# Packing two tile words for TensorE, and four block numbers for VectorE, into one register load in the relation passes of a graph network kernel

## The reference

```python
def rgcn_layer(x, src, dst, etype, W, W_root, b, num_rels):
    h = jnp.einsum('ni,rio->rno', x, W)
    msg = h[etype, src]
    seg = dst * num_rels + etype
    sums = jax.ops.segment_sum(msg, seg, num_segments=N * num_rels)
    cnt = jax.ops.segment_sum(jnp.ones(msg.shape[0], x.dtype), seg, num_segments=N * num_rels)
    mean = sums / jnp.maximum(cnt, 1.0)[:, None]
    agg = mean.reshape(N, num_rels, do).sum(axis=1)
    return agg + x @ W_root + b
# _L3_gnn_ref:
h = rgcn_layer(x, src, dst, edge_type, W1, root1, b1, NUM_RELS)
h = jax.nn.relu(h)
return rgcn_layer(h, src, dst, edge_type, W2, root2, b2, NUM_RELS)
```

## Time and profile before

| | us |
|---|---|
| Median of 3 runs | 3515.31 (3507.41 to 3517.1) |
| The profiled execution | 3496.86 |
| Its span, first to last instruction | 3494.7 |
| PE busy | 2004.6 (57%) |
| DVE busy | 1933.7 (55%) |
| POOL busy | 1461.6 (42%) |

### The profile page before, as it was taken

The page is one execution under the profiler, slowest core; times in us unless marked ns, Lnnn a source line. Parts: engine busy times, 40 slices in busy tenths (PEclk is TensorE's granted clock), DMA queues, the critical chain, the costliest instruction groups (busy, mean ns, idle before and its releaser), DMA issues.

```text
span 3494.7 us, 58674 instructions
## 1 busy us (share of the span) xinstructions
PE 2004.6 (57%) x12959; PEld 1187.5 (34%) x12959; DVE 1933.7 (55%) x6993; ACT 431.4 (12%) x904; POOL 1461.6 (42%) x1520
## 2 busy tenths in 40 slices
PE   3777799898145777777763499333333333333336
PEld 1333354444123555554531278111111111111116
DVE  5999868961345667666764466333333333333334
ACT  1555411111100000000000045000000000000000
POOL 2000000000565665556665411566656666665660
PEclk8988899999557899999985599555555555555557
DMA  2455400421112222222221111111111111111110
GB/s 69 114 114 132 109 1 1 155 81 43 48 42 54 66 68 68 66 66 68 68 57 40 36 56 74 58 43 43 43 42 44 43 43 43 43 43 41 44 43 26
DMA packets 187665, 204.28 MB, mean 58 GB/s; under 512 B 110588, under 2 KB 155277, under 8 KB 187234
## 3 DMA queue, kind: packets, MB, share of 16 engines
q0 software_dynamic: 46560, 95.32, 11.0%
q1 hardware_dynamic: 120918, 85.48, 8.9%
q10 hardware_dynamic: 19884, 19.74, 2.3%
HBM read 141.49 MB, written 39.29 MB: 52 GB/s over the span
## 4 chain that ended last, share of the span: by engine, by line
PE 41%; issue 29%; DVE 20%; another core or an unknown queue 3%; ACT 2%; SPq 1%; DVEq 1%; DMA 1%; POOL 1%; ACTq 1%; POOLq 0%
PE banks L685 16%; PE banks L660 9%; DVE hi_hot L1316 6%; DVE adj L1637 4%; PE banks L590 4%; PE banks L575 4%; PE banks L729 2%; DVE lo_hot L1324 2%; PE banks L741 2%; PE banks L776 1%; DVE zT L1620 1%; DVE hot L1611 1%; DVEq L1635 1%; DVE deg_in L1484 1%
## 5 line engine op out<-in xcount | busy, mean ns | idle before, releaser
L846 POOL DMA_INDIRECT adj<-table,adj x1453 | 1388.4, 956 | 945.8 <-SPq L462 583.0
L685 PE MATMUL banks<-adj,hot 128*128 x3908 | 776.2, 267 | 1118.4 <-issue 772.3
L1637 DVE TENSOR_TENSOR adj<-adj,banks 128x129 f32 x1954 | 564.3, 289 | 1222.1 <-PE banks L685 848.8
L685 PEld LDWEIGHTS banks<-adj,hot 128*128 128x128 f16 x3908 | 402.1, 103 | 1497.8 <-issue 1405.1
L660 PE MATMUL banks<-split,zT 128*128 128x256 f16 x2775 | 435.3, 293 | 161.9 <-DVE zT L1620 87.1
L1611 DVE TENSOR_SCALAR hot<-adj 128x128 f16<-128x128 f16 x1954 | 513.1, 263 | 1.4
L660 PEld LDWEIGHTS banks<-split,zT 128*128 128x128 f16 x2775 | 256.0, 104 | 221.3 <-issue 65.4
L547 PE MATMUL banks<-hi_hot,lo_hot 128*128 128x400 f16 x977 | 248.2, 383 | 100.7 <-DVE hi_hot L1316 64.4
L1620 DVE TENSOR_TENSOR zT<-zT,blocks 128x640 f16<-128x640 f16 x555 | 269.3, 485 | 0.0
L1316 DVE TENSOR_SCALAR hi_hot<-iota,zT 128x400 f16<-128x400 f16 x977 | 254.5, 331 | 21.0 <-PE banks L547 20.9
L590 PE MATMUL banks<-adj,split 128*128 128x512 f16 (+1 forms) x1078 | 216.8, 359 | 0.0
(11 more groups left out here) (252 smaller groups left out, 1549.4 us busy)
## 6 DMA issues: line engine op xcount, KB each, us to landing
adj<-table,adj POOLq DMA_INDIRECT x1453
adj_copy<-adj SPq DMA_DIRECT2D x24, 800.0 KB, 3.9
zT<-scr_sources ACTq DMA_DIRECT2D x111, 160.0 KB
adj<-adj_copy SPq DMA_DIRECT2D x6, 2176.0 KB, 15.9
table<-adj SPq DMA_DIRECT2D x25, 512.0 KB, 2.6
adj<-adj_copy SPq DMA_DIRECT2D x1, 3072.0 KB, 10.4
adj<-adj_copy SPq DMA_DIRECT2D x3, 1024.0 KB, 15.4
table<-split SPq DMA_DIRECT2D x6, 256.0 KB, 2.3
```

The source lines that it names most:

```text
L685: m = e.matmul(bank[j % NSUM][:, 0:b - a], hot[:, j % NHOT, :], edge[:, a:b], start=(q == 0), stop=(q == 1), skip_group_check=True)
L846: e.indirect_dma_start(gath[:, (t + which) % NG, 0:2 * D], None, table, bass.IndirectOffsetOnAxis(ap=index[:, which, t:t + 1].bitcast(U32) ...
L1637: e.tensor_tensor(a, a, bank[j % NSUM][:, 0:D + 1], ALU.add).then_inc(accumulated, 1)
```

## The change

The plan now packs the words before they go to DRAM. Two 16-bit tile words make one 32-bit word (`pairs_i`, 489 of them), and four block numbers of 8 bits make one (`quads_i`, 245). This is done by eight DVE instructions on one partition after the last `expand`, and two small memsets before it; SP's writes of the two lists wait for them (`pairs_set`). In the passes PE loads 8 registers every 16 steps, DVE 8 registers every 32 steps. Each step then cuts its field out: PE shifts (on odd steps) and masks with 0xFFFF, then masks the tile number; the maximum with 1 is gone. DVE shifts (on three steps of four) and masks. SP's `relay` and POOL's gathers are as before.

```diff
+    JP, JQ = -(-JA // 2), -(-JA // 4)
...
             e.wait_ge(rows_set, len(PICKS))
             e.dma_start(scr_c, out_c[:, :]).then_inc(plan_out, 16)
-            e.dma_start(scr_w, rows_i[:, 0, :]).then_inc(plan_out, 16)
-            e.dma_start(scr_t, rows_i[:, 1, :]).then_inc(plan_out, 16)
+            e.wait_ge(pairs_set, 2)
+            e.dma_start(scr_w, quads_i).then_inc(plan_out, 16)
+            e.dma_start(scr_t, pairs_i).then_inc(plan_out, 16)
...
             def scatter(which):
                 base = which * JA
                 for j in range(JA):
-                    if j % WORDS == 0:
-                        n = min(WORDS, JA - j)
-                        e.load(tile_regs[0:n], tile_row[:, j:j + n])
+                    w = j // 2
+                    if j % (2 * WORDS) == 0:
+                        n = min(WORDS, JP - w)
+                        e.load(tile_regs[0:n], tile_row[:, w:w + n])
                     if which == 0:
                         select_part(j)
-                    e.reg_alu(least, tile_regs[j % WORDS], (1 << BUF_LOG2) - 1, ALU.bitwise_and)
-                    e.reg_alu(least, least, 1, ALU.max)
+                    word = tile_regs[w % WORDS]
+                    if j % 2:
+                        e.reg_alu(field, word, 16, ALU.logical_shift_right)
+                        word = field
+                    e.reg_alu(field, word, 0xFFFF, ALU.bitwise_and)
+                    e.reg_alu(least, field, (1 << BUF_LOG2) - 1, ALU.bitwise_and)
                     e.wait_ge(hot_set, base + j + 1)
                     e.wait_ge(landed[which], least)
                     if which:
                         c = e.snap(least, min_val=1, max_val=T) % NG
                     else:
-                        word = e.snap(tile_regs[j % WORDS], min_val=1, max_val=((NG + NGX) << BUF_LOG2) - 1)
+                        word = e.snap(field, min_val=1, max_val=((NG + NGX) << BUF_LOG2) - 1)
                         c = word // (1 << BUF_LOG2)
...
             expand(len(PICKS) - 1)
+            fields = rows_i[:, 1, 0:2 * JP].rearrange("a (j h) -> a j h", h=2)
+            e.wait_ge(sums_read, len(PICKS))
+            e.wait_ge(own_dve, own.n)
+            e.tensor_scalar(high_i, fields[:, :, 1], 16, None, ALU.logical_shift_left).then_inc(own_dve, 1)
+            e.wait_ge(own_dve, own.up())
+            e.tensor_tensor(pairs_i, fields[:, :, 0], high_i, ALU.bitwise_or).then_inc(pairs_set, 1)
+            windows4 = rows_i[:, 0, :].rearrange("a (j h) -> a j h", h=4)
+            for h in range(1, 4):
+                e.tensor_scalar(parts_i[:, h, :], windows4[:, :, h], 8 * h, None, ALU.logical_shift_left).then_inc(own_dve, 1)
+                own.up()
+            e.wait_ge(own_dve, own.n)
+            e.tensor_tensor(parts_i[:, 0, :], windows4[:, :, 0], parts_i[:, 1, :], ALU.bitwise_or).then_inc(own_dve, 1)
+            e.wait_ge(own_dve, own.up())
+            e.tensor_tensor(parts_i[:, 1, :], parts_i[:, 2, :], parts_i[:, 3, :], ALU.bitwise_or).then_inc(own_dve, 1)
+            e.wait_ge(own_dve, own.up())
+            e.tensor_tensor(quads_i, parts_i[:, 0, :], parts_i[:, 1, :], ALU.bitwise_or).then_inc(pairs_set, 1)
...
-            regs = [e.alloc_register(f"window{i}") for i in range(REGS)]
+            regs = [e.alloc_register(f"window{i}") for i in range(WORDS)]
+            field = e.alloc_register("window_field")
...
                 for j in range(JA):
-                    if j % REGS == 0:
-                        n = min(REGS, JA - j)
-                        e.load(regs[0:n], win[0:1, j:j + n])
+                    w = j // 4
+                    if j % (4 * WORDS) == 0:
+                        n = min(WORDS, JQ - w)
+                        e.load(regs[0:n], win[0:1, w:w + n])
                     e.wait_ge(scattered, base + j + 1)
                     if j:
                         e.wait_ge(accumulated, base + j)
-                    c = e.snap(regs[j % REGS], min_val=0, max_val=NW - 1)
+                    word = regs[w % WORDS]
+                    if j % 4:
+                        e.reg_alu(field, word, 8 * (j % 4), ALU.logical_shift_right)
+                        word = field
+                    e.reg_alu(field, word, 0xFF, ALU.bitwise_and)
+                    c = e.snap(field, min_val=0, max_val=NW - 1)
```

More of the change, by code:

```diff
@@ L111, in gnn_stack @@
         adj_copy = nc.dram_tensor("adj_copy", [NB, P, NP], F16, kind="Internal").ap()
-        scr_w = nc.dram_tensor("scr_windows", [1, JA], I32, kind="Internal").ap()
-        scr_t = nc.dram_tensor("scr_tiles", [1, JA], I32, kind="Internal").ap()
+        scr_w = nc.dram_tensor("scr_windows", [1, JQ], I32, kind="Internal").ap()
+        scr_t = nc.dram_tensor("scr_tiles", [1, JP], I32, kind="Internal").ap()
         scr_l = nc.dram_tensor("scr_last", [T], I32, kind="Internal").ap()
@@ L178, in gnn_stack @@
         out_c = carve([P, JA])
-        rows_i = carve([1, 2, JA], I32)
+        rows_i = carve([1, 2, 4 * JQ], I32)
+        quads_i = carve([1, JQ], I32)
+        parts_i = carve([1, 4, JQ], I32)
+        pairs_i = carve([1, JP], I32)
+        high_i = carve([1, JP], I32)
         last_f = carve([P, TB])
@@ L232, in gnn_stack @@
         spare = rows[:, :, :].rearrange("p k d -> p (k d)")
-        win, tile_row, last_row = (spare[32 * i:32 * i + 1, 0:n].bitcast(I32) for i, n in enumerate((JA, JA, T)))
+        win, tile_row, last_row = (spare[32 * i:32 * i + 1, 0:n].bitcast(I32) for i, n in enumerate((JQ, JP, T)))
         assert JA <= 9 * D and T <= 9 * D
@@ L308, in gnn_stack @@
         selected, part_summed, copied = (sem(n) for n in ("selected", "part_summed", "copied"))
-        squared, square_sum, bound_set, bound_root, scale_set, w_high, w_low = (
-            sem(n) for n in ("squared", "square_sum", "bound_set", "bound_root", "scale_set", "w_high", "w_low"))
+        pairs_set, squared, square_sum, bound_set, bound_root, scale_set, w_high, w_low = (
+            sem(n) for n in ("pairs_set", "squared", "square_sum", "bound_set", "bound_root", "scale_set", "w_high", "w_low"))
         row_scaled, row_turned, row_high, row_low, x_turned, x_high, x_low = (
@@ L649, in _ @@
             least = e.alloc_register("least_landed")
+            field = e.alloc_register("field")
             def select_part(j):
@@ L1289, in _ @@
                         expand(c - 1)
-            expand(len(PICKS) - 1)
+            if JA % 4:
+                e.memset(rows_i[:, 0, JA:4 * JQ], 0).then_inc(own_dve, 1)
+                own.up()
+            if JA % 2:
+                e.memset(rows_i[:, 1, JA:2 * JP], 1).then_inc(own_dve, 1)
+                own.up()
+            expand(len(PICKS) - 1)
+            fields = rows_i[:, 1, 0:2 * JP].rearrange("a (j h) -> a j h", h=2)
[7 more added lines that the diff above has]
+                e.tensor_scalar(parts_i[:, h, :], windows4[:, :, h], 8 * h, None, ALU.logical_shift_left).then_inc(own_dve, 1)
+                own.up()
+            e.wait_ge(own_dve, own.n)
[4 more added lines that the diff above has]
+            e.tensor_tensor(quads_i, parts_i[:, 0, :], parts_i[:, 1, :], ALU.bitwise_or).then_inc(pairs_set, 1)
             pad = win_pad[:, :, :].rearrange("p a b -> p (a b)")
```

## The result

The changed kernel takes 3580.69 us (median of 4 runs, 3568.52 to 3588.41) against 3516.2 for the kernel before on the same chip (4 runs, 3507.41 to 3522.09): ratio 1.0179, 95% interval 1.0154 to 1.0204. That is 64 us slower, well beyond the 0.3% that a measurement can tell. The profiled execution is the fastest, 3568.52 us, with a span of 3566.4: 71.7 more than before.

The account below looks back on a forecast made before the run. Gathers were taken to set the pace of both passes by slowing PE's sequencer. Steps +10, DVE's loads -5 and plan +3 gave +8 us on 3515, so 3523 us, "no difference", range 3450 to 3590.

Parts of the forecast that it names:

- the two slower rivals: In the passes: every sequencer instruction costs (3583 us), or DVE's addition comes too late (3559 us); chance 0.18 each.
- Plan, +3 (2 to 4): End of the plan: eight DVE packing instructions on one partition add 2.8 us, taken as +3, between 2 and 4.
- PE's shift 0.088 us, a load every sixteenth step: PE in both passes: 976 shifts cost +86 us, 122 fewer loads at 0.64 us give -78, together +8.
- DVE's loads 0.59 us: DVE in the passes: 62 loads shrink from 2.10 to 0.59 us, -94 us of sequencer time, of which -5 counted.
- The waiting for one-hots: Sign in the second pass: PE's waits for DVE's one-hots fall below 70.8 us, with no gain from it.
- the term of the steps, +10: Both passes: PE's extra step work, +3 us scaled by time or +18 by instruction count, taken as +10; DVE's instructions left out.
- the late-addition rival: In the passes: DVE's masks and shifts between PE's product and the addition delay it, +41 us, 3559; chance 0.18.
- The sign that the prediction named for it: In the passes: if DVE's addition comes too late, PE's waits for additions grow by tens of microseconds.
- Loads count in full: Rival in the passes: fewer, smaller loads on PE and DVE save time, -83 us in full, -40 likelier, 3475; chance 0.28.
- Every sequencer instruction counts: Rival in the passes: each added instruction costs, whichever engine issues it, +65 us, 3583 with the plan; chance 0.18.
- The fit: Both passes: pace is a price per gather, 1.28 us, plus one per step, 0.22 us, fitted to three windows.
- 20g + 6s = 27: Window 2216 to 2243 us: 20 gathers at g and 6 steps at s fill 27 us; g = 1.28, s = 0.22.

Follow-up runs that it names:

- `no_max_b`: The kernel before without PE's maximum with 1, 1954 register instructions fewer, against the kernel before: 3447.12 against 3493.97 us, ratio 0.9863.
- PE's half: The changed kernel with DVE's half undone (DVE loads 32 whole block numbers), against the kernel before: ratios 0.9996, 0.9998 and 1.0001, kernel before at 3021 to 3025 us.
- `cut_early_b`: The changed kernel with DVE's shift and mask moved ahead of its waits, against the kernel before: 3538.94 against 3491.15 us, ratio 1.0137.
- `cut_early`: The changed kernel with DVE's shift and mask moved ahead of its waits, in an earlier set, against the kernel before: 3020.08 against 3024.9 us, ratio 0.9986.

## Why the prediction missed

It said 3523 us, "no difference"; it is 3581, slower, inside the range (3450 to 3590) but near its end. The range took it in because it had been drawn wide enough for the two slower rivals; the forecast's own, 3508 to 3535, did not, and of the +64 us it had +8. That the number lies inside is no merit of the mechanism that was forecast.

**Plan, +3 (2 to 4): right.** The first one-hot of the matrix stage starts at 85.77 instead of 82.02, +3.75. DVE's timeline at the end of the plan, behind the earlier trace rows:

```profile
77.79 0.40 DVE L1312 TENSOR_SCALAR adj<-adj 1x489 int32<-1x489 int32 x1 [0.22 <-DVE adj L1289]
78.23 0.66 DVE L1314 TENSOR_TENSOR adj<-adj 1x489 int32<-1x489 int32 x1
78.82 0.92 DVE L1317 TENSOR_SCALAR adj<-adj 1x245 int32<-1x245 int32 x3
79.77 0.58 DVE L1320 TENSOR_TENSOR adj<-adj 1x245 int32<-1x245 int32 x1
...
81.25 0.37 DVE L1327 CAST zT<-adj 1x244 int32<-1x244 f32 x1
```

From 77.50 to 81.25, 3.75 us: the shift took 0.44 to the next start (0.33 estimated), the OR 0.59 (0.58), the three shifts 0.95 (0.87), and the last three ORs 1.48 (1.05), each of which waits for the one before. The other 0.29 lie ahead of the shift, mostly a wait of 0.22 for DVE's instruction before it, which the estimate had not.

**PE's shift 0.088 us, a load every sixteenth step: right.** PE's timeline in the second pass, as in the earlier trace rows:

```profile
2616.70 0.42 PE L697 MATMUL banks<-adj,hot 128*128 x2 [0.37 <-SPq L471]
2617.39 0.41 PE L697 MATMUL banks<-adj,hot 128*128 x2 [0.27 <-SPq L471]
2618.17 0.42 PE L697 MATMUL banks<-adj,hot 128*128 x2 [0.37 <-DVE hot L1646]
2618.86 0.41 PE L697 MATMUL banks<-adj,hot 128*128 x2 [0.27 <-SPq L471]
...
2621.12 0.42 PE L697 MATMUL banks<-adj,hot 128*128 x2 [0.37 <-SPq L471]
2622.47 0.41 PE L697 MATMUL banks<-adj,hot 128*128 x2 [0.92 <-DVE hot L1646]
```

Steps of 0.69 and 0.78 us in turn, so a shift costs 0.09; the step with a load 1.35. PE's undisturbed account is even, as worked out, and the two windows without gathers agree (18 and 19 steps in 14 us).

**DVE's loads 0.59 us: right, worth nothing that shows.** Eight registers take 597 ns, 75 ns each. The Trainium skill's figure (Runtime: NRT & Kernel Launch, "Instruction fetch mechanics"), some 200 ns a register, would make it 1.6 us; the trace does not agree. The Trainium skill gives it in that section beside the register loads that the runtime injects, and these are the kernel's own, from the core's memory, so what the prediction called a contradiction may be a figure for another load. The waiting for one-hots, which was to fall below 70.8 us, rose (2280 to 3430 us):

```profile
POOL adj L858 <- SPq L468: 312.3, 219, 3.6
...
PE banks L697 <- SPq L471: 120.5, 353, 1.4
PE banks L697 <- DVE hot L1646: 88.8, 156, 1.9
PE banks L697 <- DVE adj L1678: 13.8, 24, 1.4
```

The same view of the kernel before has, beside the earlier trace rows:

```profile
PE banks L685 <- SPq L465: 72.5, 217, 1.3
...
PE banks L685 <- DVE adj L1637: 39.2, 55, 1.4
```

**The step that failed: the term of the steps, +10.** It was put together as a choice between +3 (by PE's undisturbed time) and +18 (by instructions), with the sentence "DVE's instructions I leave out of it: its 67 ns never stretch". Measured, the passes lost 66 us of the span. Two errors are in it. First, PE's time was the wrong unit. On the 3500 level a register instruction removed from PE is worth 24 ns (`no_max_b`), close to what the count gave, 0.22 / 10.4 = 21 ns, while undisturbed it is 0.09 us of PE's pace and on the 3022 level nothing. PE's own 854 more (976 shifts less 122 loads, a load counted as one) are at that price +21 us; this is inferred, since PE's half never ran on the 3500 level, and a load may weigh more than an instruction. Second, DVE's could not be left out: `cut_early_b` puts some 16 us (4 to 28) on their late place, which was the late-addition rival, priced at 41. The sign that the prediction named for it did not show: PE's waits for additions fell, from 39.2 us to 13.8. What rose are PE's waits for one-hots, by 18 us, and more than these its waits for SP's word that a tile has landed, by 48. The first went away with the early cut, and are the likely way of this part of the loss. The second did not (148.0 us in 1150 of `cut_early_b`); they probably come back to PE by way of POOL, whose gathers start later when buffers come free later. But one-hots are also waited for longer in `no_max_b` (168.2 us in both passes), which is faster, so such a sum alone proves no loss.

The account is then +3.75 (plan), +21 (PE), +16 (late place) of the 64 to 66 measured. About 23 us are left, and they lie in `cut_early_b` too, 48 - 3.75 - 21, give or take 11 by its interval alone. They fit the 3418 instructions on DVE at some 7 ns each wherever they stand, but no run shows that, and a higher price on PE would fit as well. So the cause is measured for the place, inferred for PE's number, and open for a third of the loss.

**The rivals.** "Loads count in full", 3475, has fallen: gathers for 100 us fell to 61.8, and of the kernels with fewer or smaller loads only `cut_early` was faster beyond its interval, by 0.14% on the 3022 level, where the change itself was not. "Every sequencer instruction counts", +65 and 3583, named the right signal (62 or less) and came within 2 us. It is not thereby shown as it was put: one price of 15 ns for each, 0.22 / 14.4, is less than what PE's measured (20 to 29), and DVE's, place aside, seem to cost less. Its sum came right with the parts divided otherwise.

**The fit.** Its first window was misread. In 2216 to 2243 us of the kernel before PE did not have "little to wait for", and POOL did not issue "without a pause":

```profile
2222.44 0.41 PE L685 MATMUL banks<-adj,hot 128*128 x2 [5.32 <-SPq L465]
2229.47 0.27 PE L685 MATMUL banks<-adj,hot 128*128 x1 [6.62 <-SPq L465]
...
2236.00 0.94 POOL L846 DMA_INDIRECT adj<-table,adj  x1 [1.89 <-SPq L462]
```

Of these 27 us PE's matmuls stood 19.1 waiting for SP's word that a tile had landed, so the six steps do not show that gathers slow PE itself down; they show that it waited for the relay. 20g + 6s = 27 gave g = 1.28, and g has stood up, as POOL's own pace of 1.248 us. s has no such meaning. It is POOL's standing still, spread over the steps: 0.22 before, with g kept at 1.28 (1100 - 680 x 1.28) / 851 = 0.27 in the change, (1000 - 655 x 1.28) / 821 = 0.20 in `no_max_b`, and none is left to see on the 3022 level. The prediction held it constant but for a share that it scaled by PE's time, and that is where it went wrong.

**Left open.** Why the same program takes 3022 or 3500 us, and what stretches the register instructions on the 3500 level. The records show them beside gathers only: of the 574 register, move and address instructions over 0.2 us of the kernel before, on PE and SP, each begins less than 3 us after the end of a gather or during one. But on the 3022 level the gathers are denser and none is stretched. So "gathers slow PE's sequencer down" is at most half of it: another condition, which no run here set or took away, has to be there. Two candidates stand untested. Every execution timed here, at both levels, was also profiled (each has a span and a granted clock on record). So profiling alone does not make the 3500 level, but that it has a part in the stretches is not excluded, and a price by the number of instructions would fit it. And the instructions themselves come by two DMA queues beside the gathers' (157 and 177 packets in the pages of the change, the same at both levels).

## What to carry to other kernels

Trading loads for register arithmetic trades a cost in few places for one in every step. Count the instructions that a step gains, on the engine that makes a product and on the one that consumes it, and put field extraction ahead of the wait, where it cost some 16 us less here (4 to 28). Look for unstretched and stretched records of one register instruction (minimum, median and maximum of a line): if the maximum is far above the median, price an added instruction by removing one such from each step and timing that, not by its record. And time such an edit on several occasions: this one is worth 0.0% or 1.8% by what the kernel before does in the same set.

## What was not expected of the hardware

- The kernel before took 3490 to 3522 us in four sets and 3021 to 3025 in five, with nothing between. On the 3022 level no shift or mask of PE in the rows above was over 42 ns, on the 3500 level up to 1152 ns, and most of the long ones between 0.68 and 0.73 us.
- A register operation is 32 to 36 ns on PE and 45 ns on DVE by the records. Removed from PE's steps it gave back 24 ns on the 3500 level each and nothing measurable on the 3022 level.
- Of DVE's register operations one shift of 1464 was stretched, to 700 ns, and only in the kernel in which they stood ahead of their wait.
